# An attention and mixture-of-experts layer: expert inputs transposed by one VectorE block transpose instead of four TensorE transposes

## The reference

```python
scores = jax.nn.softmax(xt @ Wg.T, axis=-1)              # xt: layernorm(x), 2048 x 512
# 2 of 4 groups of experts are kept, and 4 of 16 experts for each token
h = jax.nn.silu(jnp.einsum('td,eid->eti', xt, W1)) * jnp.einsum('td,eid->eti', xt, W3)   # inner size 352
expert_out = jnp.einsum('eti,edi->etd', h, W2)
y = jnp.einsum('etd,te->td', expert_out, combine)
z = jax.nn.silu(xt @ Ws1.T) * (xt @ Ws3.T) @ Ws2.T       # shared expert, inner size 704
x = x + (y + z)
```

## Time and profile before

| | us |
|---|---|
| median of 3 runs (1152.54 to 1153.33) | 1152.55 |
| span of the profiled execution, first to last instruction | 1150.5 |
| outside the span, taken as the difference of the two | 2.05 |
| PE busy | 1044.1 (91%) |
| DVE busy | 419.7 (36%) |
| ACT busy | 295.1 (26%) |
| POOL busy | 423.2 (37%) |

### The profile page before, as it was taken

How to read it: one execution, slowest core, us unless ns; L and a number is a source line. 1 busy time by engine, 2 the same in 40 slices (tenths; PEclk the granted TensorE clock), 3 DMA queues, 4 the chain that set the end, 5 groups by cost and what they waited for, 6 DMA issues and landing times.

```text
span 1150.5 us, 18806 instructions
## 1 busy us (share of the span) xinstructions
PE 1044.1 (91%) x5512; PEld 860.3 (75%) x5513; DVE 419.7 (36%) x857; ACT 295.1 (26%) x581; POOL 423.2 (37%) x318
## 2 busy tenths in 40 slices
PE   5899999699859996999999999999999999979993
PEld 2345555256558995888988888898888888969993
DVE  3332222477646331222222222222222222214887
ACT  2232222133312221222322223232222323212220
POOL 0000000355105888044435553355555240041664
PEclk9899999799969998999999999999999999989997
DMA  5449950044445774444424444444444222153776
GB/s 174 170 160 399 391 219 1 28 138 152 135 170 177 263 250 178 142 150 149 152 78 158 157 150 150 150 150 151 160 157 152 73 73 73 46 173 112 230 207 183
DMA packets 68603, 183.52 MB, mean 160 GB/s; under 512 B 8032, under 2 KB 8032, under 8 KB 65632
## 3 DMA queue, kind: packets, MB, share of 16 engines
q1 hardware_dynamic: 53744, 99.55, 25.3%
q0 software_dynamic: 14832, 83.63, 21.2%
HBM read 111.85 MB, written 71.30 MB: 159 GB/s over the span
## 4 chain that ended last, share of the span: by engine, by line
PE 88%; DVE 4%; DMA 3%; issue 3%; ACT 1%; POOL 0%; SPq 0%; DVEq 0%; POOLq 0%; ACTq 0%
PE ps L697 13%; PE ps L698 12%; PE ps L699 12%; PE ps L562 9%; PE ps L714 7%; PE ps L716 7%; PE ps L715 7%; PE ps L642 5%; PE ps L621 5%; PE ps L578 5%; PE ps L612 3%; DMA xq<-x_in 1%; PE ps L606 1%; DMA xg<-xn_d 1%; PE ps L601 1%
## 5 line engine op out<-in xcount | busy, mean ns | idle before, releaser
L697 PE MATMUL ps<-whi,xhi 128*128 (+1 forms) x896 | 300.8, 336 | 21.2 <-issue 15.7
L698 PE MATMUL ps<-wlo,xhi 128*128 (+1 forms) x896 | 291.0, 325 | 0.0
L699 PE MATMUL ps<-whi,xlo 128*128 (+1 forms) x896 | 290.6, 324 | 0.0
L697 PEld LDWEIGHTS ps<-whi,xhi 128*128 128x128 f32 x896 | 170.5, 190 | 27.7 <-issue 23.2
L872 DVE TENSOR_TENSOR hx<-ps,sg 128x352 f32<-128x352 f32 x112 | 58.7, 525 | 342.1 <-ACT sg L524 342.0
L698 PEld LDWEIGHTS ps<-wlo,xhi 128*128 128x128 f32 x896 | 170.8, 191 | 0.0
L699 PEld LDWEIGHTS ps<-whi,xlo 128*128 128x128 f32 x896 | 170.3, 190 | 0.0
L524 ACT ACTIVATE sg<-ps 128x352 f32<-128x352 f32 x112 | 52.0, 464 | 393.8 <-PE ps L699 393.8
L714 PE MATMUL ps<-whi,hhi 128*128 (+1 forms) x336 | 143.3, 426 | 3.8 <-DVE hlo L885 3.8
L716 PE MATMUL ps<-whi,hlo 128*128 (+1 forms) x336 | 132.6, 395 | 0.0
L715 PE MATMUL ps<-wlo,hhi 128*128 (+1 forms) x336 | 132.4, 394 | 0.0
(11 more groups left out here) (133 smaller groups left out, 1217.4 us busy)
## 6 DMA issues: line engine op xcount, KB each, us to landing
raw<-wexp_in POOLq DMA_DIRECT2D x18, 2176.0 KB, 9.6
xslot_d<-zero SPq DMA_DIRECT2D x10, 2048.0 KB, 21.7
xg<-xslot_d SPq DMA_DIRECT2D x80, 256.0 KB, 2.8
yslot_d<-ysb SPq DMA_DIRECT2D x80, 256.0 KB, 2.1
xg<-xn_d SPq DMA_DIRECT2D x32, 256.0 KB, 3.6
head_in<-heads_in POOLq DMA_DIRECT2D x4, 1152.0 KB, 8.4
xq<-x_in SPq DMA_DIRECT2D x16, 256.0 KB, 2.8
gate_d<-gate_out SPq DMA_DIRECT2D x16, 256.0 KB, 2.1
```

The source lines that it names most:

```text
L697: pe.matmul(ps[:, 2 + m, 0:INTER], xh, wh, start=(k == 0), stop=False)
L698: pe.matmul(ps[:, 2 + m, 0:INTER], xh, wl, start=False, stop=False)
L699: mm = pe.matmul(ps[:, 2 + m, 0:INTER], xl, wh, start=False, stop=(k == KT - 1))
```

## The change

The four transposes on PE go. A tile's rows are loaded so that one DVE instruction, which transposes each block of 32x32 by itself, gives columns in the contraction dimension: four DMAs a tile, one for each group of 32 partitions, with runs of 128 columns (512 bytes). The rows of `W1` and `W3` are laid out on the host in the matching order. The result is in a new SBUF buffer `xt`, not in PSUM, and `x_high` and `x_low` read it there. The order changes as well: ACT does `x_high` ahead of `silu_g`, and DVE turns the tile after next (lead 2) and does `x_low` ahead of `h_mult`.

```diff
         xg = sb3("xg", [P, XG, D], F32)
+        xt = sb3("xt", [P, 2, KT * P], F32)
...
                 def fn(t, r, turn):
                     sp.wait_ge(x_tr, base + t + 1)
-                    sp.dma_start(xg[:, r, :], rows(src, t)).then_inc(xg_loaded[r], 16)
+                    blocks = rows(src, t).rearrange("(c i) (q n) -> i q c n", i=Q, q=NQ)
+                    for q in range(NQ):
+                        sp.dma_start(xg[q * Q:(q + 1) * Q, r, :].rearrange("i (c n) -> i c n", c=NQ),
+                                     blocks[:, q, :, :]).then_inc(xg_loaded[r], 16)
...
-                    act.activation(xhi[:, p, :], ps[:, p, :], ACT.Copy).then_inc(x_hi, 1)
+                    act.activation(xhi[:, p, :], xt[:, p, :], ACT.Copy).then_inc(x_hi, 1)
...
-            pipeline(act, NR, [(0, silu_g(NT)), (1, x_high(NT)), (-1, y_evac), (0, h_high(NT))])
+            pipeline(act, NR, [(1, x_high(NT)), (0, silu_g(NT)), (-1, y_evac), (0, h_high(NT))])
...
-            def tr_x(base):
-                def fn(t, r, turn):
-                    p = r % 2
-                    pe.wait_ge(xg_loaded[r], 16 * (base // XG + turn + 1))
-                    if base or type(t) is not int or t >= 2:
-                        pe.wait_ge(x_lo, base + t - 1)
-                    transposes(ps[:, p, :], xg[:, r, :], KT, x_tr)
-                return fn
...
-                pipeline(pe, tiles, [(0, up(base, which))] + extra + [(1, tr_x(base)), (-1, down(base, which)), (0, tr_h(base))],
+                pipeline(pe, tiles, [(0, up(base, which))] + extra + [(-1, down(base, which)), (0, tr_h(base))],
...
+            def x_turn(base):
+                def fn(t, r, turn):
+                    p = r % 2
+                    dve.wait_ge(xg_loaded[r], 16 * NQ * (base // XG + turn + 1))
+                    if base or type(t) is not int or t >= 2:
+                        dve.wait_ge(x_lo, base + t - 1)
+                    dve.transpose(xt[:, p, :], xg[:, r, :].rearrange("p (c k j) -> p k c j", c=NQ, k=KT)).then_inc(x_tr, 1)
+                return fn
...
-                    dve.tensor_tensor(xlo[:, p, :], ps[:, p, :], xhi[:, p, :].bitcast(F32), ALU.subtract).then_inc(x_lo, 1)
+                    dve.tensor_tensor(xlo[:, p, :], xt[:, p, :], xhi[:, p, :].bitcast(F32), ALU.subtract).then_inc(x_lo, 1)
...
-            pipeline(dve, NR, [(0, h_mult(NT)), (1, x_low(NT)), (0, h_low(NT))])
+            pipeline(dve, NR, [(2, x_turn(NT)), (1, x_low(NT)), (0, h_mult(NT)), (0, h_low(NT))], ring=XG)
-            pipeline(dve, NT, [(0, h_mult(NT + NR)), (1, x_low(NT + NR)), (-1, add_shared(NT + NR)), (0, h_low(NT + NR)), (-4, combine)], ring=GR)
+            pipeline(dve, NT, [(2, x_turn(NT + NR)), (1, x_low(NT + NR)), (0, h_mult(NT + NR)), (-1, add_shared(NT + NR)), (0, h_low(NT + NR)), (-4, combine)], ring=GR)
```

More of the change, by code:

```diff
@@ L19 @@
 ST = S // P
+Q = 32
+NQ = P // Q
 TOK = B * S
@@ L545, in y_evac @@
                 act.activation(ysb[:, p, :], ps[:, 5 + p, :], ACT.Copy).then_inc(y_out, 1)
-            pipeline(act, NT, [(0, silu_g(0)), (1, x_high(0)), (0, h_high(0))])
-            pipeline(act, NR, [(0, silu_g(NT)), (1, x_high(NT)), (-1, y_evac), (0, h_high(NT))])
-            pipeline(act, NT, [(0, silu_g(NT + NR)), (1, x_high(NT + NR)), (0, h_high(NT + NR))])
+            pipeline(act, NT, [(1, x_high(0)), (0, silu_g(0)), (0, h_high(0))])
+            pipeline(act, NR, [(1, x_high(NT)), (0, silu_g(NT)), (-1, y_evac), (0, h_high(NT))])
+            pipeline(act, NT, [(1, x_high(NT + NR)), (0, silu_g(NT + NR)), (0, h_high(NT + NR))])
         @block.tensor
@@ L555, in _ @@
             pe.sem_inc(s1_mm, 2)
-            pe.sem_inc(x_tr, XG)
             pe.sem_inc(mm1, 2)
@@ L775, in _ @@
             pipeline(dve, NT, [(2, norm_1), (0, keep_1)], ring=XR)
+            dve.sem_inc(x_tr, XG)
             dve.wait_ge(qdec_loaded, 16)
@@ L1000, in _ @@
             r_groups()
-            pipeline(dve, NT, [(0, h_mult(0)), (1, x_low(0)), (-1, add_shared(0)), (0, h_low(0)), (0, route)])
-            pipeline(dve, NR, [(0, h_mult(NT)), (1, x_low(NT)), (0, h_low(NT))])
-            pipeline(dve, NT, [(0, h_mult(NT + NR)), (1, x_low(NT + NR)), (-1, add_shared(NT + NR)), (0, h_low(NT + NR)), (-4, combine)], ring=GR)
+            pipeline(dve, NT, [(2, x_turn(0)), (1, x_low(0)), (0, h_mult(0)), (-1, add_shared(0)), (0, h_low(0)), (0, route)], ring=XG)
+            pipeline(dve, NR, [(2, x_turn(NT)), (1, x_low(NT)), (0, h_mult(NT)), (0, h_low(NT))], ring=XG)
+            pipeline(dve, NT, [(2, x_turn(NT + NR)), (1, x_low(NT + NR)), (0, h_mult(NT + NR)), (-1, add_shared(NT + NR)), (0, h_low(NT + NR)), (-4, combine)], ring=GR)
 def constants():
@@ L1043, in pieces, with blocked @@
     def pieces(w1, w3, w2):
-        up = np.stack([w1.T.reshape(KT, P, INTER), w3.T.reshape(KT, P, INTER)], axis=2)
+        def blocked(w):
+            return w.T.reshape(NQ, KT, Q, INTER).transpose(1, 0, 2, 3).reshape(KT, P, INTER)
+        up = np.stack([blocked(w1), blocked(w3)], axis=2)
         down = np.zeros((IC * P, D), w2.dtype)
```

## The result

| | kernel before | changed kernel |
|---|---|---|
| median, range (4 runs each) | 1152.9, 1152.5 to 1153.7 us | 1189.6, 1184.4 to 1194.4 us |
| ratio, 95% interval | | 1.031, 1.028 to 1.035 |
| profiled execution, its span | 1152.55, 1150.5 us | 1184.43, 1182.8 us |

The change is slower by 3.1%: more than forecast (1164) and beyond the range (1149 to 1184).

A forecast was written before the change was run, and what follows sets the result against it. PE was taken as the bound (88% of the chain), apart from waits such as that for POOL's scatter. Sum: -26.0 + 36.4 + 1.7 + 1.1 - 1.9 = +11.3 us, forecast 1163.9 us, range 1149 to 1184.

The forecast's parts named there:

- The block: Phase 2: x_low, now with two SBUF inputs, waits for POOL's whole 6.28 us subtraction; a stall of 4.7 us at x_low.
- Rival 1: The block at x_low is short or absent: 1127 us, chance 0.17; something between, about 1145, chance 0.07.
- Stalls: Phase 2: 15 delays reaching PE, 8 ahead of a pass start at 2.8 us, 7 others at 2.0: +36.4 us.
- The saving: Phase 2 (the 80 routed tiles): transposes taken off PE give 0.44 us at each of 59 tiles, -26.0 us.
- T: Time of the new DVE transpose of one 128x512 tile, put at 0.69 us between bounds of 0.52 and 1.38.
- The clock: PE's granted clock falling after idle stretches at phase 2 stalls: nothing in the sum, +14 us only as rival 2.
- rival 2: The clock falls at the eight stalls before a pass start, eight times 1.75, +14 us: 1178; chance 0.10.
- Phase 1: First shared half, 16 tiles: no saving, as PE waits for the scatter; zero, with -2 to +3 for its start.
- rival 4: Phase 2: tile loads arrive late beside POOL's weight loads, some 9 us at each of 14: 1290; chance 0.03.
- Entries and phase 3: Phase 2 start +2.1 less 0.4, phase 3 start +1.3 less 0.2; phase 3 itself (second shared half) -1.9 us, DVE-bound.

The follow-up runs named there:

- e2_order: Changed kernel with h_mult put ahead of x_low again on DVE, x_low keeping two SBUF inputs: 1184.1 us, 0.988 of the kernel before.
- e1_psum: Changed kernel with the transposed tile written to PSUM instead of SBUF, so x_low has one input in each: 1170.0 us, 0.980 of the kernel before.
- e8_long: e7_late with an added DVE reduction (5 repeats of 512 columns) ahead of h_mult of each pass's fourth tile in phase 2: 1263.8 us, one run.
- e4_fill: Changed kernel with two added matmuls ahead of tr_h of each pass's fourth tile in phase 2: 1225.1 us, one run.
- a_again: Changed kernel, unchanged, run again beside the kernel before: 1188.8 us, 1.031 of the kernel before.
- the second pair of traces: Kernel before and changed kernel, both unchanged, traced again on one chip: 1149.7 us (one run) and 1188.8 us.
- e5_plain: e1_psum with one load of 2 KB runs a tile in place of four of 512-byte runs, only its time of use: 1128.8 us, 0.979.
- e7_late: e1_psum with x_turn listed behind x_low on DVE in all three phases: 1130.2 us, 0.981 of the kernel before.
- e3_pieces: Changed kernel with POOL's subtractions cut into four and three pieces: 1170.3 us, 0.982 of the kernel before.
- e9_pieces: Changed kernel with POOL's subtractions in pieces and x_turn behind x_low on DVE: 1178.9 us, 0.978 of the kernel before.

## Why the prediction was wrong

- **The block, right.** 15 rows near 5 us, 0.55 us behind POOL; forecast 4.7 us of delay, measured 4.7 (5.31 against 0.65). Rival 1 fell: the hold is that of the whole POOL instruction. What no row had shown is that POOL's casts hold as well (e2_order).
- **Stalls, right.** 8 + 7 of them; by the passes 8 x 2.7 + 7 x 2.2 = 37, forecast 36.4.
- **The saving, right.** 26.0 in phase 2, by e1_psum. T is 0.70 us, forecast 0.69; that it is so near is luck, as the bounds were 0.52 and 1.38.
- **The clock, the step that failed.** The price, +14, stood under rival 2 with a chance of 0.10, set aside because "neither of the two idle stretches at a stall is that long". In the sum the clock stood at nothing. Phase 2 grew by 25.5 us: -26.0 + 37 leaves 14.5, nine to ten falls of 1.5. The trace had shown a fall behind a longer stand, and I took its length for a threshold, which no row bore out. e8_long shows that 1.8 and 1.9 us with half a microsecond of work between are enough, and e4_fill that one alone can be. How often the clock falls also differs from run to run: nine stretches at 0.50 in the first trace and ten in a_again, whose phase 2 is 3.4 us longer; and the four runs of the changed kernel spread over 10 us, the kernel before over 1.2. Why it falls behind one stretch and not behind another of the same length stays open.
- **Phase 1, failed too.** Put at 0, bounds -2 to +3; up to the first load of phase 2 it cost 5.2 us (8.2 from the first load in the second pair of traces). Of that 3.7 stand ahead of the first `up`: the loads beside POOL's weight loads were weighed for phase 2 alone (rival 4), and e5_plain shows that the four loads make the first tile late. Another 1.9 lie in the scatter, which was put at no change; what makes it longer isn't shown.
- **Entries and phase 3, right.** Phase 2's entry 7.7 against 5.4, +2.3 (forecast 2.1): its first `x_low` takes 1.58 us and ends 0.56 behind POOL's subtraction, as foreseen. Phase 3's entry +1.2 (1.3; 1.6 in the second pair of traces); phase 3 itself -1.8 (-1.9), with `h_mult` every 6.75 to 7.1 us in its middle, as DVE became the bound:

```profile
1121.17 0.51 DVE L869 TENSOR_TENSOR hx<-ps,sg 128x352 f32<-128x352 f32 x1
...
1127.92 0.51 DVE L869 TENSOR_TENSOR hx<-ps,sg 128x352 f32<-128x352 f32 x1
```

With +14.5 for the clock and +5.2 for phase 1 the forecast of 1163.9 becomes 1183.6; the profiled run took 1184.4. It was the fastest of the four, and the median, 1189.6, is 5 us more. The other three left no trace, but over a whole run their mean granted clock was lower (0.947, 0.945 and 0.943 against 0.950), the lower the longer the run. In the second pair of traces, whose spans are 39.4 us apart, phase 2 has 29.4 of it and phase 1 8.2.

## What to carry to other kernels

An instruction moved to DVE must be priced with its operands' memory: a second SBUF input cost whatever was left of the GpSimd instruction that was running, up to 4.7 us here and 1.6 in e2_order. Keeping one input in PSUM (e1_psum 0.980, e7_late 0.981) or cutting GpSimd's instruction (e3_pieces 0.982) turned 3% slower into 2% faster. Put what can be blocked behind what the bound engine waits for, not ahead of it. When stalls open idle stretches near 2 us on TensorE, put falls of the clock into the sum or its range, instead of setting them aside because a stretch is shorter than the last one seen.

## What was not expected of the hardware

- The granted clock fell to 0.50 in e8_long after stands of about 1.8 and 1.9 us with 0.5 of work between, each of 19 times; after a single stand of 1.8 to 1.9 us it fell 9 times of 15 in e4_fill, and once and twice of seven in the two traces of the changed kernel.
- The same kernel takes 1152.9, 1192.4 or 1204.5 us on different chips. In phase 1 of e1_psum, beside the scatter, ACT's `silu` starts 8.4 us after its tile's `up` ended (388.13); the profile names only a remote releaser:

```profile
396.51 0.46 ACT L529 ACTIVATE sg<-ps 128x352 f32<-128x352 f32 x1 [8.52 <-remote]
```

What holds it there stays open.
- POOL's subtraction in four pieces takes 7.1 us in place of 6.3 (e9_pieces), and between the pieces DVE gets in at once: there the piece behind `x_low` takes 2.15 us and the others 1.7, so 0.45 of the extra time is POOL's own wait.
- In the changed kernel each of the 15 long `x_low` ended 0.55 us behind POOL's instruction, and in e2_order each of the 15 ended as far behind a cast.
